# Folding half of an adjacency tile onto the other before it is packed into bits

## The chip, the cores and the metric

The kernel runs on one core of a Trainium2 chip. The metric is the device time of one execution in microseconds. The core has five engines that run their own instruction streams in order and wait for each other on semaphores: TensorE (PE; its weight loads are PEld), VectorE (DVE), ScalarE (ACT), GpSimd (POOL) and SyncE (SP), which here issues the loads.

## What is computed

A graph network of four layers on 4096 nodes with 256 features and one adjacency matrix of 4096 x 4096 int32. Each layer is attention over the neighbours, with a residual sum and a layer norm. Layers 0 and 1 (four heads of 64 features) are what the change touches, with the adjacency matrix's way into the chip:

```
h = x @ W;  e[i, j] = leaky_relu(s_src[i] + s_dst[j])      # per head
e = where(adj == 0, -inf, e)
out = softmax(e, axis=j) @ h
x = layernorm(x + out)
```

Layers 2 and 3 are of the same kind with other score functions and more dense algebra; they read the same adjacency matrix.

## The kernel before

The 4096 rows of the adjacency matrix are 32 tiles t of 128 rows. Each comes in two halves of 128 x 2048 int32 (1 MB) into `adj_in[:, half]`, one buffer for each half, so that SyncE loads half h of tile t only when half h of tile t-1 has been read. **convert(t, half)** (L1724) is one VectorE compare that writes the half as bf16 zeros and ones into `adj_bf[:, t % 2, half]`. **pack_half** (L1320) is 16 TensorE matmuls on 128 x 128 slices of one half against `powers`, identities scaled by powers of two: eight slices add up to a byte, so 32 matmuls (two halves) make a tile's 128 x 512 bytes in one PSUM bank. **store_packed** (L1730 on VectorE for the first tiles, L945 on ScalarE for the others) writes them into `packed`, which stays on the chip for all four layers.

Where this work stands: seven tiles (`PACKED_FIRST`) are converted before attention. Tiles 0 to 4 are packed between the quads of layer 0's projection; `dense(l, q)` is quad q of eight, four tiles of 128 nodes (L1308 with eight score columns appended to the 256 features; L1290 are the transposes for the next quad), whose results ScalarE copies out of PSUM (L876 features, L877 scores). Tiles 5 and 6 are packed after the last quad. The others go three to a **group**: a group is 512 destination nodes of one head, eight units k of 64 matmuls (L1377 and L1380). For every unit VectorE makes two masks (`masks`: edge L1799, pos L1804, neg L1807, in buffers for two units) from the bytes and from `above`, which ScalarE makes (L974). In layer 0's first groups, at = 0 to 7, VectorE has the six converts of three tiles in its program at k = 0 to 5, and TensorE has half a tile's packing after its units k = 1 to 6. Group 8 takes tile 31.

Between projection and first group stands a transition. `masks_ahead` makes the masks of two units; `stats` (L1931 to L1938) takes the largest score and subtracts it, ScalarE raises two exponentials (L909, L910); `first_products` (L1825), `first_rests` (L1834) and `first_lasts` (L1840) make the first attention values in three bf16 parts, with ScalarE's casts (L958) between. Then TensorE starts group 0.

The order on each engine is written out by hand; no scheduler moves anything. The functions that the change touches:

Of the kernel before, what the change touches and what calls it, by code (L numbers as in the profile page):

```python
# [7 lines left out]
ALU = mybir.AluOpType  # L8
# [63 lines left out]
PACKS = 3  # L72

# [100 lines left out]
def gnn_kernel(nc, A, out, last_layer=3):  # L174

    with ExitStack() as ctx:
# [164 lines left out]
        s_hps = sem("h_in_psum")  # L341
        s_h = sem("h_made")
# [228 lines left out]
        def first_tiles(l, u):  # L571

            out = []
            for kind, vtmp in enumerate((vtmp_dve, vtmp_pool)):
                j = slice(u * CHUNK, (u + 1) * CHUNK)
                factor, hd = (emul[:, kind, 0:1, j], 0) if l < 3 else (emul[:, 0, 1:2, j], kind)
                k0 = kind * kind_step(l)
                part = [values[:, 0, j, k0 + i * C:k0 + (i + 1) * C] for i in range(PARTS)]
                out.append((vtmp, factor.rearrange("p a n -> p n a"), h[:, j, hd * D:(hd + 1) * D], part))
            return out  # L580
# [284 lines left out]
        def _(act):  # L865
# [5 lines left out]

            def copy_quad_h(l, q):

                for i in range(QT):
                    act.wait_ge(s_hps, q * QT + (l * T + i + 1))
                    act.activation(h[:, q * QT + i, :], bank[2 + i][:, 0:F], ACT.Copy)  # L876
                    act.activation(scores[:, :, q * QT + i], bank[2 + i][:, F:F + 2 * H], ACT.Copy).then_inc(s_h, 1)  # L877
                    if i % 2 == 1 and q + 1 < QUADS:
                        copy_xT_half(l, q + 1, i // 2)
# [20 lines left out]
            def stats(l):  # L900
# [350 lines left out]
            for l in range(last_layer + 1):  # L1251
# [5 lines left out]
                if l < 3:  # L1257
                    for half in range(2):
                        copy_xT_half(l, 0, half)
                    for q in range(QUADS):  # L1260
                        if l == 1 and q in (0, 2):
                            elu_exp(AHEAD + 3 + q // 2)
                        if l < 2 and q == ROW_AT + 1:
                            copy_row(l)
                        if l < 2 and q > ROW_AT:
                            above_ahead(l, q - ROW_AT - 1)
# [14 lines left out]
        def _(pe):  # L1281
# [11 lines left out]

            def dense(l, q):
# [19 lines left out]
            def pack_half(t, half, b):  # L1314

                pe.wait_ge(s_adjbf, t * 2 + half + 1)
# [46 lines left out]
            def group(l, slot, par, at, packs=(), first=False):  # L1363

                for k in range(BITS):
# [20 lines left out]
                    if 1 <= k <= 2 * len(packs):  # L1386
                        n, half = divmod(k - 1, 2)
                        if half == 0:
# [3 lines left out]
                            else:  # L1392
                                pe.wait_ge(s_banksum, PACKS * (at - 1) + n + 1)
                        pack_half(packs[n], half, GT * (1 - par) + n)
# [292 lines left out]
        def _(dve):  # L1687
# [31 lines left out]
            def convert(t, half):  # L1719

                dve.wait_ge(s_adj[half], (t + 1) * 16)
                if t >= 2:
                    dve.wait_ge(s_packmm, t * 2 + half - 3 + CREDIT)
                dve.tensor_scalar(adj_bf[:, t % 2, half, :], adj_in[:, half, :], 0, None, ALU.is_gt)\  # L1724
                    .then_inc(s_adjbf, 1)
# [83 lines left out]
            def masks_ahead(l):  # L1809
# [4 lines left out]
                for k in range(UNITS_AHEAD):  # L1814
                    for _ in masks(l, TURN[l] * H * UNITS + k, k, packed[:, :, 0:WORDS]):
                        pass

            def first_products(l, u):
# [3 lines left out]
                for vtmp, factor, columns, _ in first_tiles(l, u):  # L1822
# [102 lines left out]
            def stats(l):  # L1925

                n = H if l < 3 else 1
                if l < 3:
                    dve.wait_ge(s_h, T * (l + 1) + 1)
# [73 lines left out]
            def group(l, g, gg, par, banks_before, norm=None, first=False, front=None, fold=None, ahead=None,  # L2003
# [7 lines left out]
                for k in range(BITS):  # L2011
# [14 lines left out]
                    if l == 0 and first and k == 0:  # L2026
                        store_packed(PACKED_WOVEN, 6 + PACKED_WOVEN % 2)
# [14 lines left out]
                    elif k < UNITS_AHEAD:  # L2042
                        if k == 0:
                            first_rests(l, 0)
                            first_lasts(l, 0)
                    else:
# [373 lines left out]
            for l in range(last_layer + 1):  # L2420
                if l == 3:
                    dense2()
                if l == 0:
                    fold_first_weights()
                    for t in range(PACKED_FIRST):
                        for half in range(2):
                            convert(t, half)
# [37 lines left out]
```

## Time and profile before

| what | value |
|---|---|
| time, median of 3 runs | 2997.62 us (2996.97 to 2999.9) |
| the profiled execution: its own time, its span | 2995.74 us, 2993.9 us |
| TensorE matmuls busy | 2923.0 us, 98% of the span |
| VectorE busy | 2133.9 us, 71% |
| ScalarE busy | 1920.6 us, 64% |
| adjacency loads | 64 of 1 MB, median 4.9 us from issue to landing |

The profile is one execution. A share is an average over the span: VectorE's 71% holds stretches of layer 0 where it works nearly all the time, and others where it has little to do. A row of a timeline gives the start, the duration and, in brackets, how long the engine sat idle before it and what it then waited for.

### The profile page before, as it was taken

How to read it: one execution, taken by the hardware profiler on the slowest of the kernel's cores; microseconds unless marked ns; L12 is line 12 of the kernel's file. 1: busy time of each engine (PE TensorE's matmuls, PEld its weight loads, DVE VectorE, ACT ScalarE, POOL GpSimd, SP SyncE). 2: the span in 40 equal slices, each digit the busy share in tenths (PEclk: the TensorE clock that was granted, in tenths of full speed). 3: DMA queues.
4: the chain of work that ended last, by engine and by line, in shares of the span. 5: the costliest groups of instructions: out<-in, count | busy, mean ns of one | idle time of the engine just before them, and what ended most of it. 6: DMA issues, size and time to landing. Idle time of an engine off the chain costs nothing.

```text
span 2993.9 us, 65253 instructions
## 1 busy us (share of the span) xinstructions
PE 2923.0 (98%) x24628; PEld 2556.9 (85%) x24628; DVE 2133.9 (71%) x3887; ACT 1920.6 (64%) x3414; POOL 1179.6 (39%) x1559
## 2 busy tenths in 40 slices
PE   7999999999989999999999999999999999989999
PEld 6899999999979999999998878887788878755555
DVE  5999898888888888888896556566666656562245
ACT  4777999999988999999985545444455444430000
POOL 0672385641226565654121023333323333444222
PEclk9999999999999999999999999999999999999999
DMA  8677100000100000000010000000000000000001
GB/s 292 207 234 246 39 11 15 11 11 14 62 15 13 11 15 11 15 11 15 11 35 12 4 1 4 4 1 4 1 4 4 1 1 1 3 1 1 0 14 42
DMA packets 41912, 104.55 MB, mean 35 GB/s; under 512 B 9856, under 2 KB 23424, under 8 KB 33536
## 3 DMA queue, kind: packets, MB, share of 16 engines
q1 hardware_dynamic: 39616, 101.61, 10.4%
q8 instruction: 111, 1.82, 0.2%
q10 hardware_dynamic: 2112, 0.52, 0.1%
q14 instruction: 73, 0.60, 0.1%
HBM read 97.73 MB, written 4.39 MB: 34 GB/s over the span
## 4 chain that ended last, share of the span: by engine, by line
PE 89%; DVE 5%; ACT 2%; issue 2%; DMA 1%; POOL 1%; SPq 0%; DVEq 0%; POOLq 0%; ACTq 0%
PE bank L1377 21%; PE bank L1380 21%; PE bank L1435 16%; PE bank L1473 13%; PE bank L1383 11%; PE bank L1308 2%; PE bank L1462 2%; DMA arena<-in_adj_dram 1%; PE bank L1449 1%; DVE rings L1804 1%; DVE arena L1724 1%; PE bank L1320 1%; ACT above L974 1%; PE bank L1358 1%; DVE rings L1799 1%
## 5 line engine op out<-in xcount | busy, mean ns | idle before, releaser
L1377 PE MATMUL bank<-values,rings 128*128 128x195 bf16 x8192 | 1392.1, 248 | 31.5 <-DVE rings L1807 19.0
L1380 PE MATMUL bank<-values,rings 128*128 128x195 bf16 x8192 | 1392.0, 248 | 0.0
L974 ACT ACTIVATE above<-srow,kpass 128x512 fp8e4<-128x512 f32 x2032 | 1279.9, 709 | 96.2 <-DVE rings L1807 87.1
L1377 PEld LDWEIGHTS bank<-values,rings 128*128 128x128 fp8e4 x8192 | 802.9, 98 | 44.0 <-issue 39.8
L1380 PEld LDWEIGHTS bank<-values,rings 128*128 128x128 fp8e4 x8192 | 802.9, 98 | 0.4
L1804 DVE TENSOR_TENSOR rings<-rings,above 128x512 uint32<-128x512 uint32 x512 | 387.1, 756 | 171.8 <-PE bank L1380 135.4
L1062 ACT ACTIVATE values<-srow,cmul 128x512 f32<-128x512 f32 x256 | 206.0, 815 | 411.5 <-PE bank L1473 410.5
L1807 DVE TENSOR_TENSOR rings<-rings 128x512 uint32<-128x512 uint32 x512 | 425.7, 831 | 17.3
L1473 PE MATMUL bank<-hv,values 128*128 128x257 f32 x1792 | 420.6, 380 | 0.0
L1473 PEld LDWEIGHTS bank<-hv,values 128*128 128x128 f32 x1792 | 335.0, 190 | 69.9 <-issue 25.2
L1383 PE MATMUL bank<-values,rings 128*128 128x390 bf16 x1920 | 318.7, 329 | 10.1 <-DVE values L1840 10.1
L1383 PEld LDWEIGHTS bank<-values,rings 128*128 128x128 fp8e4 x1920 | 188.3, 98 | 140.5 <-issue 12.4
L633 POOL TENSOR_TENSOR quot<-sums,cmul 128x260 f32<-128x260 f32 x64 | 49.4, 771 | 563.9 <-DVE sums L1960 453.4
L1799 DVE TENSOR_SCALAR rings<-packed 128x512 uint32 (+1 forms) x512 | 260.6, 509 | 2.5 <-ACT packed L945 2.4
L1914 DVE SCALAR_TENSOR_TENSOR values<-values,cmul,rings 128x512 f32<-128x512 f32 x256 | 191.8, 757 | 35.0 <-ACT values L1062 34.4
L766 POOL TENSOR_SCALAR zrow<-zrow 128x1 f32<-128x1 f32 x128 | 45.6, 356 | 429.7 <-DVE zrow L2168 429.7
L2031 DVE TENSOR_SCALAR rings<-packed 128x512 uint32 (+1 forms) x120 | 54.4, 453 | 199.6 <-PE bank L1383 199.5
L1960 DVE TENSOR_REDUCE sums<-bank 128x130 f32<-128x390 f32 x320 | 176.5, 554 | 3.5 <-PE bank L1358 1.7
L1435 PE MATMUL bank<-arena,above 128*128 128x256 f32 (+1 forms) x496 | 165.9, 482 | 0.8 <-ACT above L1117 0.8
L1435 PEld LDWEIGHTS bank<-arena,above 128*128 128x128 f32 x496 | 94.0, 190 | 53.1 <-issue 43.8
L1435 PE MATMUL bank<-quot,arena 128*128 128x256 f32 x512 | 118.3, 379 | 0.0
L562 POOL TENSOR_TENSOR values<-vtmp_pool,values 128x260 f32 (+1 forms) x112 | 105.9, 946 | 21.9 <-POOL values L559 14.5
(223 smaller groups left out, 3483.5 us busy)
## 6 DMA issues: line engine op xcount, KB each, us to landing
arena<-in_adj_dram SPq DMA_DIRECT2D x64, 1024.0 KB, 4.9
srow<-src_dram SPq DMA_DIRECT2D x69, 256.0 KB, 3.1
x<-in_x_dram SPq DMA_DIRECT2D x4, 1024.0 KB, 11.4
out_dram<-x SPq DMA_DIRECT2D x7, 512.0 KB, 2.9
arena<-in_L_gnn_fe_w_dram SPq DMA_DIRECT2D x2, 512.0 KB, 7.2
arena<-in_L_gnn_W_hz_dram SPq DMA_DIRECT2D x1, 1024.0 KB, 7.7
arena<-in_L_gnn_g_w_dram SPq DMA_DIRECT2D x1, 1024.0 KB, 10.9
weights<-in_L_gnn_W_dram SPq DMA_DIRECT2D x3, 256.0 KB, 3.5
```

The source lines that it names most:

```text
L974: last = act.activation(above[:, k % 2, q, :], srow[:, par, :], ACT.Relu, scale=BIG, bias=kpass[:, p % 2, k * Q + q:k * Q + q + 1], satura ...
L1062: act.activation(w2[:, m % DEPTH, :], srow[:, g % 2, :], ACT.Relu, scale=b_col[:, jt:jt + 1], bias=c_neg[:, jt:jt + 1]).then_inc(E.relu, 1)
L1377: pe.matmul(acc[:, 0:KW], pos[:, k % 2, q, :].bitcast(FP8)[:, rows], v[:, 0:KW], start=start, stop=final, skip_group_check=True)
L1380: last = pe.matmul(acc[:, KP:KP + KW], neg[:, k % 2, q, :].bitcast(FP8)[:, rows], v[:, KP:KP + KW], start=False, stop=final, skip_group_ch ...
L1383: last = pe.matmul(acc[:, 0:2 * KW], edge[:, k % 2, q, :].bitcast(FP8)[:, rows], v[:, 0:2 * KW], start=start, stop=final)
L1435: last = pe.matmul(dst, lhsT[k], rhs[k], start=(k == 0), stop=(k == len(lhsT) - 1))
L1473: last = pe.matmul(bank[it][:, 0:VW], w2[:, m % DEPTH, it * P:(it + 1) * P], hv[:, k * Q + q, :], start=(k == 0 and q == 0), stop=False)
L1799: dve.tensor_scalar(edge[:, r], words, shift[0], ONE, shift[1], ALU.bitwise_and).then_inc(s_dve, 1)
L1804: dve.tensor_tensor(pos[:, r], edge[:, r], above[:, r].bitcast(U32), ALU.bitwise_and).then_inc(s_dve, 1)
L1807: dve.tensor_tensor(neg[:, r], edge[:, r], pos[:, r], ALU.bitwise_xor).then_inc(s_sides, 1)
L1914: dve.scalar_tensor_tensor(out=w2[:, m % DEPTH, :], in0=w2[:, m % DEPTH, :], scalar=c_pos[:, jt:jt + 1], in1=edge[:, unit % 2, q, :].bitca ...
L1960: return dve.tensor_reduce(sums[:, slot, it, :, :], parts, AX.X, ALU.add)
```

## The change

Thirteen tiles (0 to 6, and 22, 23, 25, 26, 28, 29) are **folded**. Half 0 is converted as before but scaled by 2^-4. Half 1 is no longer converted by itself: one VectorE instruction (`scalar_tensor_tensor`, called the fold here) compares it and adds the result onto the bf16 tile of half 0, so that each element holds two bits. TensorE then packs 16 slices of that one tile instead of 32, and waits for both halves. In the groups it does so after unit k = 2n+2 for the n-th tile of the group, and nothing after k = 2n+1.

In layers 0 and 1 the last quad's scores are computed by matmuls of their own, 8 columns wide, into bank 6: those of the quad's first two tiles ahead of its features, those of the other two behind the first tile's features. ScalarE copies all four tiles' scores with one instruction, and `stats` waits for that copy instead of for the last features. Bank 6 holds packed tile 4 just before, so in layer 0 these matmuls wait for its store. Tile 6's converts move from ahead of the masks into the transition, `masks_ahead` makes one unit's masks, the second unit's come behind `first_lasts`, and the products start behind the first of the two exponentials. The two stores of the transition stand at its end.

```
+FOLDED_LATE = (22, 23, 25, 26, 28, 29)
+DOWN_HALF = 2.0 ** -(BITS // 2)
+def folded(t):
+    return t < PACKED_FIRST or t in FOLDED_LATE
...
+            def copy_last_scores(l):
+                act.wait_ge(s_scoreps, l + 1)
+                act.activation(scores[:, :, T - QT:T], bank[6][:, 0:QT * 2 * H].rearrange("p (t c) -> p c t", c=2 * H),
+                               ACT.Copy).then_inc(s_lastscores, 1)
...
-                    act.activation(e[:, 1], e[:, 0], ACT.Exp, scale=SLOPES[l])
+                    act.activation(e[:, 1], e[:, 0], ACT.Exp, scale=SLOPES[l]).then_inc(s_expone, 1)
...
+            def scores_first(l, q, tiles):
+                if l == 0:
+                    pe.wait_ge(s_packed, (PACKED_WOVEN - 1) // 2 * 2 + 1 + CREDIT)
+                for i in tiles:
+                    pe.wait_ge(s_xt, q * 2 + (l * 2 * QUADS + i // 2 + 1))
+                    for k in range(2):
+                        last = pe.matmul(bank[6][:, i * 2 * H:(i + 1) * 2 * H], xT[q % 2][:, i, k, :],
+                                         weights[:, k, F:F + 2 * H], start=(i == 0 and k == 0),
+                                         stop=(i == QT - 1 and k == 1), skip_group_check=True)
...
+                last_quad = q == QUADS - 1 and l < 2
+                if last_quad:
+                    scores_first(l, q, (0, 1))
+                    width = F
                 for i in range(QT):
+                    if last_quad and i == 1:
+                        scores_first(l, q, (2, 3))
...
-                pe.wait_ge(s_adjbf, t * 2 + half + 1)
+                pe.wait_ge(s_adjbf, t * 2 + (2 if folded(t) else half + 1))
+                if folded(t):
+                    for k in range(half * (BITS // 4), (half + 1) * (BITS // 4)):
...
+                if folded(t) and half == 0:
+                    dve.tensor_scalar(adj_bf[:, t % 2, 0, :], adj_in[:, 0, :], 0, DOWN_HALF, ALU.is_gt, ALU.mult)\
+                        .then_inc(s_adjbf, 1)
+                elif folded(t):
+                    dve.wait_ge(s_adjbf, t * 2 + 1)
+                    dve.scalar_tensor_tensor(out=adj_bf[:, t % 2, 0, :], in0=adj_in[:, 1, :], scalar=0,
+                                             in1=adj_bf[:, t % 2, 0, :], op0=ALU.is_gt, op1=ALU.add)\
+                        .then_inc(s_adjbf, 1)
...
                     shifted.then_inc(s_shift, 1)
-                    dve.wait_ge(s_exps, l + 1)
+                    if l == 0:
+                        convert(PACKED_FIRST - 1, 0)
+                    dve.wait_ge(s_expone, l + 1)
...
                     if l == 0 and first and k == 0:
-                        store_packed(PACKED_WOVEN, 6 + PACKED_WOVEN % 2)
+                        convert(PACKED_FIRST - 1, 1)
...
                             first_lasts(l, 0)
+                            for _ in masks(l, unit + 1, 1, words):
+                                pass
+                            if l == 0:
+                                store_packed(PACKED_WOVEN, 6 + PACKED_WOVEN % 2)
```

On VectorE, the transition of layer 0 in the kernel before, from the largest score to tile 7's converts (`arena<-arena`; `packed<-bank` are the stores, `values` and `vtmp_pool` the two kinds of first values):

```order
L1938 TENSOR_TENSOR emul<-scores,smax 128x128
L2023 MEMSET credits 128x1
L1824 COPY values<-emul 128x8
L1825 TENSOR_TENSOR values<-hv,emul 128x8x64
L1824 COPY vtmp_pool<-emul 128x8
L1825 TENSOR_TENSOR vtmp_pool<-hv,emul 128x8x64
L1730 CAST packed<-bank 128x4x128
L1834 TENSOR_TENSOR values<-values 128x520
L1834 TENSOR_TENSOR vtmp_pool<-vtmp_pool,values 128x520
L1840 TENSOR_TENSOR values<-values 128x8x65
L1840 TENSOR_TENSOR values<-vtmp_pool,values 128x8x65
L1730 CAST packed<-bank 128x4x128
```

The same place in the changed kernel:

```order
L2003 TENSOR_TENSOR emul<-scores,smax 128x128
L1777 TENSOR_SCALAR arena<-arena 128x2048
L2090 MEMSET credits 128x1
L1888 COPY vtmp_pool<-emul 128x8
L1889 TENSOR_TENSOR vtmp_pool<-hv,emul 128x8x64
L1888 COPY values<-emul 128x8
L1889 TENSOR_TENSOR values<-hv,emul 128x8x64
L1781 SCALAR_TENSOR_TENSOR arena<-arena 128x2048
L1898 TENSOR_TENSOR vtmp_pool<-vtmp_pool,values 128x520
L1898 TENSOR_TENSOR values<-values 128x520
L1904 TENSOR_TENSOR values<-vtmp_pool,values 128x8x65
L1904 TENSOR_TENSOR values<-values 128x8x65
```

Tile 6's compare and fold now stand inside the transition, and the two stores (and the second unit's three mask instructions) come behind these rows.

On TensorE, the last two quads of layer 0's projection in the changed kernel, behind tile 4's packing; the 128x8 rows are the scores by themselves, and the x32 at the end the packing of tiles 5 and 6:

```order
L1360 MATMUL bank<-powers,arena 128x128 x16
L1347 MATMUL bank<-weights,values 128x264 x4
L1310 MATMUL bank<-ident,x 128x128 x4
L1347 MATMUL bank<-weights,values 128x264 x4
L1310 MATMUL bank<-ident,x 128x128 x4
L1321 MATMUL bank<-weights,values 128x8 x4
L1347 MATMUL bank<-weights,values 128x256 x2
L1321 MATMUL bank<-weights,values 128x8 x4
L1347 MATMUL bank<-weights,values 128x256 x6
L1396 MATMUL bank<-ident,scores 128x128
L1360 MATMUL bank<-powers,arena 128x128 x32
```

Before, the same place read x32 for tile 4, eight matmuls of 264 columns for the last quad, and x64 for tiles 5 and 6.

On VectorE, inside group 5 of layer 0, from tile 22's fold to tile 23's; `rings` are the masks, `sums` a reduction of the group before:

```order
L1781 SCALAR_TENSOR_TENSOR arena<-arena 128x2048
L1860 TENSOR_SCALAR rings<-packed 128x512
L1865 TENSOR_TENSOR rings<-rings,above 128x512
L1868 TENSOR_TENSOR rings<-rings 128x512
L2027 TENSOR_REDUCE sums<-bank 128x130
L1777 TENSOR_SCALAR arena<-arena 128x2048
L1860 TENSOR_SCALAR rings<-packed 128x512
L1865 TENSOR_TENSOR rings<-rings,above 128x512
L1868 TENSOR_TENSOR rings<-rings 128x512
L2027 TENSOR_REDUCE sums<-bank 128x130
L1781 SCALAR_TENSOR_TENSOR arena<-arena 128x2048
```

Each of the two folds stands where a compare stood, ahead of the masks of k = 2 and of k = 4; nothing else moved on VectorE there.

## Rows read from the trace of the kernel before

**Rows 1.** The page's first part, and its chain that ended last, by engine.

```profile
PE 2923.0 (98%) x24628; PEld 2556.9 (85%) x24628; DVE 2133.9 (71%) x3887; ACT 1920.6 (64%) x3414; POOL 1179.6 (39%) x1559
...
PE 89%; DVE 5%; ACT 2%; issue 2%; DMA 1%; POOL 1%; SPq 0%; DVEq 0%; POOLq 0%; ACTq 0%
```

**Rows 2.** Stretches of layer 0: length, busy PE, PEld, DVE, ACT, POOL, clock, DMA.

```profile
100.00:150.00 50.00, 45.26 (x577) 43.87 (x574) 48.79 (x59) 37.85 (x63) 42.49 (x53) 1.00 0.57 186
...
233.40:260.30 26.90, 26.90 (x356) 26.90 (x353) 23.90 (x35) 21.48 (x35) 5.45 (x5) 1.00 0.75 245
```

**Rows 3.** What VectorE waits for, 20 to 63 and 74 to 206 us.

```profile
DVE arena L1724 <- DMA arena<-in_adj_dram: 26.7, 14, 3.9
...
DVE rings L1799 <- ACT packed L945: 2.4, 1, 2.4
...
DVE rings L1804 <- PE bank L1380: 0.2, 1, 0.2
```

**Rows 4.** The chain of waits, 20 to 64 us: start, us, what.

```profile
50.52 4.75 DMA arena<-in_adj_dram
...
55.30 1.24 DVE arena L1724
...
56.55 5.47 DMA arena<-in_adj_dram
```

**Rows 5.** VectorE's timeline over the transition of layer 0.

```profile
62.05 1.23 DVE L1724 TENSOR_SCALAR arena<-arena 128x2048 bf16<-128x2048 int32 x1 [2.65 <-DMA arena<-in_adj_dram]
...
66.77 0.28 DVE L1931 TENSOR_REDUCE smax<-scores 128x4 f32<-128x128 f32 x1
...
68.49 0.17 DVE L1824 COPY values<-emul 128x8 f32<-128x8 f32 x1 [0.58 <-issue]
...
70.44 0.69 DVE L1834 TENSOR_TENSOR values<-values 128x520 f32<-128x520 f32 x1
...
73.06 0.68 DVE L1730 CAST packed<-bank 128x512 uint8<-128x512 f32 x1
73.66 2.60 DVE L1724 TENSOR_SCALAR arena<-arena 128x2048 bf16<-128x2048 int32 x2
```

**Rows 6.** TensorE's timeline over the last quad and the start of group 0.

```profile
58.74 0.49 PE L1290 MATMUL bank<-ident,x 128*128 128x128 f32 x3
59.07 3.73 PE L1308 MATMUL bank<-weights,values 128*128 128x264 f32 x16
63.34 0.33 PE L1348 MATMUL bank<-ident,scores 128*128 128x128 f32 x1 [0.55 <-ACT scores L877]
...
73.25 0.32 PE L1377 MATMUL bank<-values,rings 128*128 128x195 bf16 x1 [6.00 <-issue]
```

**Rows 7.** VectorE's groups of instructions, whole span: busy us, mean ns | idle before.

```profile
L1724 DVE TENSOR_SCALAR arena<-arena 128x2048 bf16<-128x2048 int32 x64 | 80.4, 1257 | 26.7 <-DMA arena<-in_adj_dram 26.7
...
L2185 DVE SCALAR_TENSOR_TENSOR above<-vtmp_pool,above 128x512 f32<-128x512 f32 x62 | 41.2, 683 | 26.1 <-ACT vtmp_pool L1100 25.0
...
L1737 DVE SCALAR_TENSOR_TENSOR values<-values,hv 128x1024 f32<-128x1024 f32 x8 | 9.7, 1218 | 0.2 <-ACT values L893 0.2
```

**Rows 8.** VectorE's timeline in group 5: masks of k = 0, 1 and 5.

```profile
224.57 0.69 DVE L1804 TENSOR_TENSOR rings<-rings,above 128x512 uint32<-128x512 uint32 x1 [1.38 <-PE bank L1380]
...
228.49 0.69 DVE L1804 TENSOR_TENSOR rings<-rings,above 128x512 uint32<-128x512 uint32 x1 [1.03 <-ACT above L974]
...
243.53 1.11 DVE L1807 TENSOR_TENSOR rings<-rings 128x512 uint32<-128x512 uint32 x1
```

**Rows 9.** The chain of waits in group 5: half a tile packed behind unit 4.

```profile
244.16 0.89 PE bank L1320 x16
```

**Rows 10.** A short idle time of TensorE (its timeline), and the window behind it.

```profile
91.94 0.32 PE L1377 MATMUL bank<-values,rings 128*128 128x195 bf16 x1 [2.38 <-DVE rings L1807]
...
92.00:94.00 2.00, 2.00 (x13) 1.86 (x14) 1.97 (x3) 2.00 (x4) 0.00 (x0) 0.50 0.13 16
```

**Rows 11.** TensorE's timeline in layer 1's transition: the first matmul of group 0.

```profile
874.18 0.32 PE L1377 MATMUL bank<-values,rings 128*128 128x195 bf16 x1 [5.73 <-DVE values L1840]
```

More of the change, by code:

```diff
@@ L1264, in _ @@
                             copy_row(l)
+                        if l < 2 and q == QUADS - 1:
+                            copy_last_scores(l)
                         if l < 2 and q > ROW_AT:
@@ L1292, in x_across @@
                 last.then_inc(s_xtps, 1)
+            def scores_first(l, q, tiles):
[7 more added lines that the diff above has]
+                                         stop=(i == QT - 1 and k == 1), skip_group_check=True)
+                if tiles[-1] == QT - 1:
+                    last.then_inc(s_scoreps, 1)
             def dense(l, q):
@@ L1314, in pack_half @@
             def pack_half(t, half, b):
-                pe.wait_ge(s_adjbf, t * 2 + half + 1)
+                pe.wait_ge(s_adjbf, t * 2 + (2 if folded(t) else half + 1))
+                if folded(t):
+                    for k in range(half * (BITS // 4), (half + 1) * (BITS // 4)):
+                        for q in range(Q):
+                            j = k * Q + q
+                            last = pe.matmul(bank[b][:, q * P:(q + 1) * P], adj_bf[:, t % 2, 0, j * P:(j + 1) * P],
+                                             powers[:, BITS // 2 + k, :], start=(k == 0 and q == 0),
+                                             stop=(k == BITS // 2 - 1 and q == Q - 1), skip_group_check=True)
+                    last.then_inc(s_packmm, 1)
+                    return
                 for k in range(half * (BITS // 2), (half + 1) * (BITS // 2)):
@@ L1387, in group @@
                         n, half = divmod(k - 1, 2)
-                        if half == 0:
+                        if folded(packs[n]) and half == 0:
+                            continue
+                        if half == 0 or folded(packs[n]):
                             if at == 0:
@@ L1813, in masks_ahead @@
                     dve.wait_ge(s_packed, GT + CREDIT)
-                for k in range(UNITS_AHEAD):
-                    for _ in masks(l, TURN[l] * H * UNITS + k, k, packed[:, :, 0:WORDS]):
-                        pass
+                for _ in masks(l, TURN[l] * H * UNITS, 0, packed[:, :, 0:WORDS]):
+                    pass
             def first_products(l, u):
@@ L1821, in first_products @@
                     dve.wait_ge(s_vrest, first_values_before(l) + 2 * u)
-                for vtmp, factor, columns, _ in first_tiles(l, u):
+                if l < 2 and u == FIRST_CHUNKS - 1:
+                    dve.wait_ge(s_h, T * (l + 1) + 1)
+                for i, (vtmp, factor, columns, _) in enumerate(first_tiles(l, u)):
+                    if l < 2 and u == 0 and i == 1:
+                        dve.wait_ge(s_exps, l + 1)
                     big = vtmp[:, 0]
@@ L2426, in _ @@
                         for half in range(2):
-                            convert(t, half)
+                            if t < PACKED_FIRST - 1:
+                                convert(t, half)
                         if 1 <= t <= PACKED_WOVEN:
```

23 lines of the change are left out of this document (16 added, 7 removed).

## The prediction

> **What bounds the kernel now.** The page comes first: TensorE is busy for 98% of the span and holds 89% of the chain that ended last [rows 1]. By that, 7 microseconds of matmuls taken off would be 7 off the time. The share is an average, so I look next at stretches. Between 100 and 150 us TensorE works 45.26 of 50 us and VectorE 48.79; from 233.4 to 260.3, in group 5 of layer 0, it is TensorE with all of 26.90, and VectorE has 23.90 [rows 2]. So layer 0 has two parts. In the early one VectorE is the bound: from 74 to 206 us it waits in five places for 4.5 us in all, the first and last of which are 2.4 for a store by ScalarE and 0.2 for TensorE [rows 3]. In the late one TensorE is, with about 3 us of VectorE's left over in a group. Ahead of both stands the loading, 20 to 63 us, where VectorE waits 26.7 us, 14 times, for adjacency halves [rows 3]. The chain of waits there alternates between two things, a load of half 1 (six between 4.75 and 5.88, the shortest shown) and the compare of that half, 1.24 [rows 4]: the next load into the one buffer starts only when VectorE has read the last. What VectorE does with half 0 is not on this chain, and what it does with half 1 is.
>
> **What a fold costs.** The compare it takes the place of has 1.22 to 1.26 us for 2048 elements. The trace has no fold with an int32 and a bf16 source; the nearest rows are scalar_tensor_tensor with two f32 sources, 683 ns for 512 elements and 1218 for 1024 [rows 7], so 1.045 ns an element, and 1.218 + 1024 x 0.001045 = 2.29 us for 2048. From below, the fold could cost what the compare does. I take 2.29, the price of the same instruction: 1.06 more each. Seven folds stand early and six late, 13 x 1.06 = 13.8 us of VectorE's work, against 13 x 16 = 208 fewer matmuls of TensorE's, at 0.89 for 16 [rows 9] 11.6 us. The scaled compare of half 0 has one more operation on the same elements; I cost it as the compare.
>
> Both f32 rows come to about one element in a nanosecond. The Trainium skill (Vector Engine (DVE) Microarchitecture Reference, section 7, points that are easy to get wrong) says that this instruction with two sources in SBUF that are not bf16 has its throughput halved. It speaks against the change; by it, were the int32 source enough, a fold would take some 4.4 us. The L1737 row, with two f32 sources, shows 1218 ns for 1024 elements, no halving against the 512 row.
>
> **Early part, layer 0.** Fold by fold: tile 5's half 1 was ready at 55.30 [rows 4]. Five folds (tiles 0 to 4) stand ahead of its load on that chain. Were each wholly added, it comes 5.3 later; as the two halves' loads then overlap less, each load may shrink towards the shortest, by up to 0.5, which leaves 2.8. I take 0.9 a tile, 4.5: ready at 59.8 (58.1 to 60.6). Its fold ends at 62.0, and the store of tile 4 behind it takes 0.60 (from 73.06 to 73.66) [rows 5]: 62.6.
>
> TensorE comes sooner to the last quad. Tile 4's fold ends one cycle of the chain earlier (4.75 + 1.24 before, 0.9 more now), at 55.1; 16 packing matmuls, 0.9, and quad 6, 16 records at 0.223 and eight transposes at 0.11 [rows 6], 4.45, bring it to 60.4. There it has to wait for the store of tile 4, about 2.2 us, since the scores go into the same bank. What packing saves ahead of that (five times 0.9) is so spent in waiting for folds.
>
> A matmul of eight columns isn't in the trace: between nothing and the 0.22 of a record of 264 columns. I take 0.11, that of a transpose record [rows 6], 0.87 for the eight records of two tiles. From 62.6: scores 0.87, first tile 0.89, scores 0.87, so 65.3; ScalarE's copy 0.4, 65.7 (the wait for the copy was 0.55 before) [rows 6]. One unit's masks took 1.79 (two between the convert that starts at 62.05 and 66.77), so they are done. From largest score to shifted scores it was some 1.13 (from 66.77 to the start of the wait of 0.58 that ends at 68.49) [rows 5]: 66.9. Tile 6's compare stands next, 1.14, to 68.05. The exponential should have run beside it, but on ScalarE it stands behind the four feature copies, and the quad's matmuls end at 65.3 + 2.7 = 68.05. So the products start at 68.7, against 68.49: the early scores buy nothing. Products 1.35, fold of tile 6 2.2, to 72.25; rests and lasts with their gap 2.6 (from 70.44 to 73.06) [rows 5], to 74.8, where TensorE starts, against 73.25. Then the second masks, 1.8, and two stores, 1.2: tile 7's compare at 77.8 instead of 73.66. **+4.1**, from +2.4 (loads shrink all they can) to +6. It stays, since VectorE has no idle time behind it to give it back [rows 3].
>
> **Late groups.** Groups 5, 6 and 7 each have two folds. VectorE has 23.90 + 2.12 = 26.0 us of work a group, TensorE 26.9 - 1.8 = 25.1. VectorE's idle time sits at the start: 1.38 for TensorE to give back a mask buffer, 1.03 for ScalarE [rows 8]; from k = 2 on it waits for nothing. In the middle it is just in time: the masks of k = 5 end at 243.53 + 1.11 = 244.64, TensorE ends its packing behind unit 4 at 245.05 [rows 8, 9], 0.4 later. Two folds put these masks at 246.76, so unit 5 starts 1.7 later; units 6 and 7, and the next group's first wait on them, follow. The wait for ScalarE may shrink, its work being 21.48 of 26.90 [rows 2]: I take +1.4 a group, **+4.2** for three. From above: 5.7, nothing taken up and a little more. From below: VectorE without any wait, 26.0 against 26.9, is -0.9 a group, -2.6.
>
> **Layer 1** has no packing. TensorE's first group waited 5.73 us for the products [rows 11]. The scores come earlier, the exponentials still stand behind the feature copies, and 16 score records add up to 1.75; the second unit's masks, made in idle time before, come behind `first_lasts`. **+0.5**, from -0.7 to +1.5.
>
> **Sum.** 4.1 + 4.2 + 0.5 = +8.8 on the profiled execution's 2995.74 us: 3004.5. The median of the runs is 1.9 higher: **3006.4 us**. A measurement of this kernel can tell about 0.2%, 6 us, from no change.
>
> **Rivals.** *The late waits absorb the folds* (0.25): VectorE's 2.4 us of waiting in a group take the 2.1 that two folds add, as VectorE falls behind and finds buffers free. What decides is whether these waits are for something that moves along; the 1.38 is for TensorE's unit 6, which I say moves. Then a group is 26.5, -0.4, and the sum 4.1 - 1.2 + 0.5 = +3.4: 3001, not slower by what can be told.
> *The clock falls ahead of the last quad* (0.08): an idle time of 2.38 us was followed by a granted clock of 0.50 [rows 10], and I forecast one of 2.2. The projection's first matmuls at the lower of the two levels cost some 1.6 more: 3008.
> *A fold costs no more than the compare* (0.09): the early chain stays, about +0.4; the late groups are TensorE's, -1.8 each; layer 1 as above: -4.5, 2993.
> *TensorE is the bound throughout* (0.06), as its 98% says: 11.6 us of packing come off, 2986. Against it stands VectorE's 48.79 of 50.
> *The fold runs at half the pace of the f32 rows* (0.02): 2048 x 1.045 ns, 2.1 us, more than I took for each of the five early folds in the chain of loads, for tile 6's and for the six late ones, 25 us on top: 3032. The f32 rows speak against it. The Trainium skill's rule named above would be its reason.
>
> **How the numbers follow.** My forecast has 0.50, and spans 3001 to 3012 by its bounds, most of it above 3003.6, the mark of 0.2%. Slower: 0.42 of it, the clock's 0.08 and the halved fold's 0.02, 0.52. Same: the rest of the forecast 0.08, the late waits 0.25, half the cheap fold, 0.37. Faster: the other half and TensorE as the bound, 0.11. The range leaves out the cheap fold, TensorE's bound and the halved fold: 2996 to 3011.
>
> **What would show it.** The fold's row: 2.3 us. The chain of waits before 63 us with folds of 2.3 in it and loads of about 5.1; TensorE idle for some 2 us ahead of the 8-column matmuls, waiting for VectorE's store; the products at about 68.7, tile 7's compare at about 77.8. In groups 5 to 7 TensorE idle in front of units 2, 4 and 5, waiting for masks, and a period of 28.3 instead of 26.9. I am wrong if the fold's row is near 1.2, if loads shrink by as much as folds grow, or if VectorE's waits at k = 0 and k = 1 vanish and TensorE's groups come every 26.5 or less.

## The result, and the profile after

| what | before | after |
|---|---|---|
| median of the runs | 2997.63 us (2996.97 to 2999.9, 6 runs) | 3013.19 us (3010.03 to 3015.15, 6 runs) |
| ratio | | 1.005, 95% interval 1.004 to 1.006 |
| the profiled execution, its span | 2995.74 us, 2993.9 us | 3012.15 us, 3010.3 us |

Slower, by 15.6 us (0.5%) where 8.8 were forecast, and outside the range. The page after, its first part and its chain by engine, hardly differs from [rows 1]: VectorE has 14.7 us more to do. TensorE has 176 matmuls fewer (208 of packing less 32 of scores) and is busy no shorter, since more of its work ran at the lower clock, as will be seen.

```profile
PE 2924.2 (97%) x24452; PEld 2556.1 (85%) x24452; DVE 2148.6 (71%) x3887; ACT 1921.4 (64%) x3408; POOL 1180.8 (39%) x1559
...
PE 87%; DVE 7%; issue 2%; ACT 2%; DMA 1%; POOL 1%; SPq 0%; DVEq 0%; POOLq 0%; ACTq 0%
```

Where the time went is read off VectorE's timeline in both kernels: the last mask instruction of each unit (L1807, now L1868) is the n-th of its kind in either, so the difference of their starts is the delay at that place. It grows at three places. After the transition of layer 0 it is 7.97 us, 9.25 at the end of group 0 and through group 4; in each of the groups 5, 6 and 7 it grows by 2.02; at layer 1's transition by 0.83. With 0.3 behind that, it is the 16.4 by which the spans differ.

The fold's row among VectorE's groups of instructions, to be held against the compare in [rows 7]:

```profile
L1781 DVE SCALAR_TENSOR_TENSOR arena<-arena 128x2048 bf16<-128x2048 int32 x13 | 29.7, 2287 | 15.3 <-DMA arena<-in_adj_dram 15.3
```

2.287 us, where 2.29 was forecast. The chain of waits over the loading, where [rows 4] were:

```profile
53.20 2.31 DVE arena L1781
55.51 0.02 issue
55.52 4.78 DMA arena<-in_adj_dram
...
62.53 0.69 DVE packed L1791
63.23 0.04 issue
63.27 0.83 PE bank L1321 x6
```

Tile 5's half 1 came at 60.32 (59.8 forecast), and the chain goes from its fold to the store of tile 4 and from there to the 8-column matmuls on TensorE, as the prediction had it. What TensorE then did, in its timeline, and one window of that stretch with the granted clock (the third figure from the end):

```profile
63.27 1.07 PE L1321 MATMUL bank<-weights,values 128*128 128x8 f32 x8 [2.08 <-DVE packed L1791]
64.20 2.06 PE L1347 MATMUL bank<-weights,values 128*128 128x256 f32 x4
66.05 1.72 PE L1321 MATMUL bank<-weights,values 128*128 128x8 f32 x8
67.61 4.50 PE L1347 MATMUL bank<-weights,values 128*128 128x256 f32 x12
...
79.14 0.32 PE L1425 MATMUL bank<-values,rings 128*128 128x195 bf16 x1 [1.53 <-issue]
```

```profile
66.00:68.00 2.00, 2.00 (x10) 1.95 (x9) 0.00 (x0) 0.20 (x2) 0.00 (x0) 0.50 0.36 152
```

TensorE waited 2.08 us, and the clock, at 1.00 for about another microsecond, then stood at 0.50, the lower of its two levels, for most of the quad. The last quad took from 63.27 to 72.1, 8.8 us instead of the 5.45 forecast (62.6 to 68.05). VectorE's timeline, the rows that answer to [rows 5], shows that this was waited for:

```profile
68.10 0.29 DVE L1996 TENSOR_REDUCE smax<-scores 128x4 f32<-128x128 f32 x1 [3.10 <-ACT scores L885]
...
72.78 0.17 DVE L1888 COPY vtmp_pool<-emul 128x8 f32<-128x8 f32 x1 [2.40 <-issue]
...
74.13 2.28 DVE L1781 SCALAR_TENSOR_TENSOR arena<-arena 128x2048 bf16<-128x2048 int32 x1
...
82.02 2.44 DVE L1785 TENSOR_SCALAR arena<-arena 128x2048 bf16<-128x2048 int32 x2
```

It idles 3.10 us for the scores and 2.40 in front of the products, and tile 7's compare stands at 82.02: 8.4 later than in [rows 5], and 4.2 later than forecast. In group 6, VectorE's two waits (as in [rows 8]) are still there. The second is for `above`, which ScalarE makes behind its store of the group's third packed tile, and that store has itself waited for TensorE's packing (the ACT row). TensorE now has three waits of its own, ahead of units 2, 4 and 5; the window is that group's whole period:

```profile
262.74 0.69 DVE L1865 TENSOR_TENSOR rings<-rings,above 128x512 uint32<-128x512 uint32 x1 [1.38 <-PE bank L1428]
...
266.66 0.69 DVE L1865 TENSOR_TENSOR rings<-rings,above 128x512 uint32<-128x512 uint32 x1 [1.03 <-ACT above L992]
```

```profile
263.53 0.60 ACT L963 ACTIVATE packed<-bank 128x512 uint8<-128x512 f32 x1 [1.64 <-PE bank L1368]
```

```profile
272.69 0.24 PE L1425 MATMUL bank<-values,rings 128*128 128x195 bf16 x1 [1.11 <-DVE rings L1868]
280.54 0.24 PE L1425 MATMUL bank<-values,rings 128*128 128x195 bf16 x1 [1.41 <-DVE rings L1868]
...
285.08 0.24 PE L1425 MATMUL bank<-values,rings 128*128 128x195 bf16 x1 [0.79 <-DVE rings L1868]
```

```profile
262.74:291.66 28.92, 25.60 (x324) 25.05 (x322) 26.03 (x34) 21.82 (x35) 5.46 (x5) 1.00 0.67 228
```

Before, the period was 26.90, all of it TensorE's [rows 2]; now it is 28.92, with TensorE busy for 25.60; the three waits are the difference.

### The profile page after: what moved, and what is told of

Its sections match the earlier page's. It is cut to its first block, busy times and chain, and to the rows that moved or that the text cites. A ratio compares the mean times of both kernels' runs of the same rounds, so it can differ in the third digit from the quotient of the medians.

```text
span 3010.3 us, 64901 instructions
## 1 busy us (share of the span) xinstructions
PE 2924.2 (97%) x24452; PEld 2556.1 (85%) x24452; DVE 2148.6 (71%) x3887; ACT 1921.4 (64%) x3408; POOL 1180.8 (39%) x1559
## 4 chain that ended last, share of the span: by engine, by line
PE 87%; DVE 7%; issue 2%; ACT 2%; DMA 1%; POOL 1%; SPq 0%; DVEq 0%; POOLq 0%; ACTq 0%
PE bank L1425 20%; PE bank L1428 20%; PE bank L1487 16%; PE bank L1525 13%; PE bank L1431 11%; PE bank L1347 2%; PE bank L1514 2%; DVE rings L1865 2%; PE bank L1501 1%; DMA arena<-in_adj_dram 1%; ACT above L992 1%; DVE rings L1860 1%; DVE arena L1785 1%; DVE arena L1781 1%; DVE rings L1868 1%
## 5 line engine op out<-in xcount | busy, mean ns | idle before, releaser
L1868 DVE TENSOR_TENSOR rings<-rings 128x512 uint32<-128x512 uint32 x512 | 426.2, 832 | 17.3
L1431 PEld LDWEIGHTS bank<-values,rings 128*128 128x128 fp8e4 x1920 | 188.2, 98 | 140.8 <-issue 12.5
```

The costliest lines, as they stand in the source:

```text
L1431: last = pe.matmul(acc[:, 0:2 * KW], edge[:, k % 2, q, :].bitcast(FP8)[:, rows], v[:, 0:2 * KW], start=start, stop=final)
L1868: dve.tensor_tensor(neg[:, r], edge[:, r], pos[:, r], ALU.bitwise_xor).then_inc(s_sides, 1)
```

## The experiments

**Theories.** A: of the early delay, what goes beyond the forecast is the low clock in the last quad. Against it, B: only the wait for the store counts, and C: the new order of the transition is itself the cost. V: the late groups run in a loop through VectorE whose period was 26.8 us all along (28.92 less 2 x 1.06), its two waits included, just under TensorE's 26.9. Against it, S: TensorE is their bound and VectorE has time left.

For all runs together, from VectorE's timelines: the start of the last mask of unit 2 (behind the transition), that of unit 40 (the first of group 5), and the period of groups 5, 6 and 7.

| kernel | unit 2 | unit 40 | periods | median against before on the same chip |
|---|---|---|---|---|
| before | 81.45 | 225.29 | 26.91 26.91 26.90 | |
| changed | 89.42 | 234.54 | 28.92 28.93 28.92 | +15.6 |
| again | 86.57 | 231.87 | 28.93 28.93 28.92 | +14.6 |
| filled | 84.74 | 230.05 | 28.92 28.93 28.92 | +12.5 |
| other_bank | 85.39 | 230.32 | 28.93 28.93 28.93 | +9.6 |
| plain_compare | 83.60 | 227.72 | 26.79 26.81 26.79 | +2.1 |
| scores_only | 81.00 | 226.86 | 26.91 26.91 26.90 | +1.5 |
| early_only_old_transition | 87.88 | 232.50 | 26.90 26.91 27.45 | +8.7 |
| late_only | 80.22 | 224.71 | 28.92 28.93 28.93 | +5.8 |
| first_of_three | 82.04 | 227.28 | 27.87 27.87 27.87 | +3.8 |
| third_of_three | 81.31 | 225.17 | 27.62 27.68 28.05 | +3.7 |
| in_the_wait_none | 81.65 | 226.96 | 26.91 26.90 26.91 | +0.9 |
| in_the_wait_one | 80.64 | 224.40 | 26.02 26.01 26.01 | -2.0 |
| in_the_wait_two | 83.83 | 229.15 | 26.91 26.91 26.91 | +1.0 |

The periods repeat to 0.02 us within a kernel, but for third_of_three and the last one of early_only_old_transition (27.45, for which no run shows a cause). The early columns don't repeat like that: seven kernels (before, late_only and the five of the last rows) have the same program up to group 4, and unit 2 stands there between 80.22 and 83.83, unit 40 between 224.40 and 229.15, means 81.6 and 226.1. The spread is there before the transition: the last adjacency half that VectorE waits for came between 60.87 and 64.47 in these seven. A difference of 2 us in these columns, in single executions, is none.

**filled.** TensorE is kept at work while it waits, and nothing else is changed:

```
+FILL = 40
...
+                if last_quad and l == 0:
+                    pe.wait_ge(s_packed, PACKED_WOVEN - 1 + CREDIT)
+                    for n in range(FILL):
+                        pe.matmul(bank[7][:, 0:P], powers[:, 0, :], powers[:, 1, :], start=True, stop=True,
+                                  skip_group_check=True)
                 if last_quad:
                     scores_first(l, q, (0, 1))
```

Expected:

> The changed kernel, with 40 matmuls of 128 x 128 (bf16, into bank 7, which nobody reads then) ahead of the last quad's score matmuls in layer 0, so that TensorE works through most of the 2.08 us in which it now waits for tile 4's store; everything else waits as in the changed kernel. Theory A, the clock: the changed kernel's last quad ran from 63.27 to 72.1 us, 8.8 us, because the granted clock was 0.50 there; at full clock it takes 5.5. Then the products start some 3.3 earlier than 72.78, tile 7's compare stands near 78.8 instead of 82.1, and the delay of group 4's masks against the kernel before falls from 9.25 to 6 or, if the low clock of group 0 goes too, to 4.7; span 3005.5 to 3007. Theory B, the wait alone: what counts is when the store comes, and the stretched matmuls lie beside other work; then the span stays at 3010.

TensorE's timeline:

```profile
59.33 2.40 PE L1339 MATMUL bank<-powers 128*128 128x128 bf16 x40
61.93 1.06 PE L1322 MATMUL bank<-weights,values 128*128 128x8 f32 x8 [0.20 <-DVE packed L1797]
...
64.60 2.84 PE L1353 MATMUL bank<-weights,values 128*128 128x256 f32 x12
67.91 0.33 PE L1402 MATMUL bank<-ident,scores 128*128 128x128 f32 x1 [0.47 <-ACT hv L893]
```

The quad takes 61.93 to 67.4, 5.5 us, at full clock; unit 2 is 4.7 earlier than in the changed kernel. 1.3 of that is not the clock's: in this execution tile 5's half 1 came at 58.98 instead of 60.32. What is left, 3.3, is the difference in the quad's length. B falls, and the medians agree: 3.1 less than in the changed kernel. The span, 3007.8, is above the 3005.5 to 3007 expected.

**other_bank.** The scores no longer wait for tile 4's store:

```
-                    pe.wait_ge(s_packed, (PACKED_WOVEN - 1) // 2 * 2 + 1 + CREDIT)
+                    pe.wait_ge(s_packed, PACKED_WOVEN - 1 + CREDIT)
...
-                        last = pe.matmul(bank[6][:, i * 2 * H:(i + 1) * 2 * H], xT[q % 2][:, i, k, :],
+                        last = pe.matmul(bank[7 - l][:, i * 2 * H:(i + 1) * 2 * H], xT[q % 2][:, i, k, :],
```

Expected:

> The changed kernel, with the last quad's scores of layer 0 in bank 7 instead of bank 6, so that they wait for tile 3's store, long done, instead of tile 4's. Theory A, the clock: TensorE reaches the last quad at 61.2 and goes straight on at full clock, ends it at 66.7, products at about 67.4, tile 7's compare at 76.6 against 73.66 before: the early delay falls from 9.25 to about 3 to 4, span 3004 to 3005. Theory B, the wait alone: 2.1 less, span 3008.2. Rival C, the new order of the transition (tile 6's compare and fold and the second unit's masks inside it) is the main cost: the early delay stays above 6.

TensorE goes into the quad without a wait and at full clock:

```profile
61.32 0.96 PE L1321 MATMUL bank<-weights,values 128*128 128x8 f32 x8
...
63.89 2.84 PE L1347 MATMUL bank<-weights,values 128*128 128x256 f32 x12
```

Unit 2 is 4.0 earlier than in the changed kernel, unit 40 4.2; span 3007.5 where 3004 to 3005 was expected. In this execution tile 5's half 1 came only at 61.96, 1.6 later than in the changed kernel's; from there VectorE waits 0.34 us in all up to tile 7's compare at 77.99 (76.6 expected). So the delay left, 3.8 against the mean of the seven, holds the folds, the new order and that late load, and no more wait for TensorE.

**plain_compare.** Half 1 of the thirteen tiles is converted as before, and the packing stays at 16 slices, so this kernel leaves half 1's edges out of the bits:

```
-                elif folded(t):
-                    dve.wait_ge(s_adjbf, t * 2 + 1)
-                    dve.scalar_tensor_tensor(out=adj_bf[:, t % 2, 0, :], in0=adj_in[:, 1, :], scalar=0,
-                                             in1=adj_bf[:, t % 2, 0, :], op0=ALU.is_gt, op1=ALU.add)\
-                        .then_inc(s_adjbf, 1)
```

Expected:

> The changed kernel, but the second half of the thirteen tiles is converted by the plain compare of before, into its own tile; TensorE still packs 16 slices, of half 0 alone, so half 1's edges of these tiles are left out of the bits. It takes the 1.06 us of each fold away and keeps what TensorE saves. Theory V for the late groups (VectorE's own loop, with its waits at k = 0 and k = 1 that move along, has a period of 28.92 - 2.12 = 26.8 us, and TensorE's 26.9 was only just longer): the groups 5 to 7 come every 26.8, -0.1 each, although TensorE has 1.8 less to do. Rival S (TensorE is their bound and VectorE has time left): 25.1 each, -5.4 for three. Early: without the folds the chain of loads is that of before, tile 4's store is done at 57.2, the last quad ends at 62.7, tile 7's compare at 71.5 against 73.66, -2. Span by V 2992.5, by S 2987.

Period 26.8, as V had it, and not the 25.1 of S. One group's window:

```profile
254.51:281.32 26.81, 25.61 (x323) 25.06 (x321) 23.93 (x35) 21.73 (x35) 5.45 (x5) 1.00 0.74 246
```

TensorE has 1.2 us idle here and VectorE 2.9, and still the groups come no faster: neither's work alone is the period. The early part was expected 2 us ahead of before and was 2 behind (span 2998.0 for 2992.5), by the same mishap as in the changed kernel: TensorE waited for the store, and the quad ran at the low clock.

```profile
58.53 1.27 PE L1321 MATMUL bank<-weights,values 128*128 128x8 f32 x8 [2.39 <-DVE packed L1786]
...
63.06 4.31 PE L1347 MATMUL bank<-weights,values 128*128 128x256 f32 x12
```

**scores_only.** No folds:

```
 def folded(t):
-    return t < PACKED_FIRST or t in FOLDED_LATE
+    return False
```

Expected:

> The changed kernel without any fold: all tiles are converted and packed as before, and only the last quad's scores and the new order of the transition are left. Theories A and V: the chain of loads is that of before, TensorE reaches the last quad at 59.1, does not wait for tile 4's store (57.1), products at 65.2, tile 7's compare at 73.3, -0.4 against before; layer 1 +0.8; span 2994 to 2995. Rival C, the transition's new order is the main early cost by itself: tile 7's compare at 77 or later, span 2998 or more.

Products at 65.42, tile 7's compare at 73.60 against 73.66 before: C falls as a main cost. The span, 2997.1, is above the 2994 to 2995 expected, and short of C's 2998. Unit 4's masks were 0.80 behind, where unit 2's were 0.45 ahead; the changed kernel has the same step of 1.25 (7.97 to 9.22), and the kernel with the old transition has not. It is a stretch at the low clock again. TensorE's timeline at unit 2 and a window behind it, in the changed kernel, and the same place in plain_compare:

```profile
90.20 0.24 PE L1425 MATMUL bank<-values,rings 128*128 128x195 bf16 x1 [1.96 <-DVE rings L1868]
```

```profile
92.00:94.00 2.00, 2.00 (x14) 1.83 (x13) 1.97 (x3) 0.70 (x2) 0.00 (x0) 0.50 0.85 213
```

```profile
84.39 0.24 PE L1425 MATMUL bank<-values,rings 128*128 128x195 bf16 x1 [3.20 <-DVE rings L1863]
```

```profile
86.00:88.00 2.00, 2.00 (x32) 2.00 (x30) 1.97 (x3) 0.88 (x2) 0.00 (x0) 1.00 0.78 180
```

From unit 3's last mask to unit 4's it takes 7.9 to 8.1 us in the five kernels whose clock is at 0.50 there, and 6.8 in the nine where it is at 1.00: the step is the clock's. Of the six kernels with the new order, five have it; plain_compare has not, though its TensorE had waited longer. The kernel before pays the same a little later, behind its wait of 2.38 ahead of unit 4 [rows 10]. By unit 40 scores_only is within the spread of the seven.

**early_only_old_transition.** The kernel before with `convert` and `pack_half` of the change for tiles 0 to 6, and nothing else:

```
+FOLDED = (0, 1, 2, 3, 4, 5, 6)
+def folded(t):
+    return t in FOLDED
```

Expected:

> The kernel before with tiles 0 to 6 folded and nothing else of the change: the last quad has its scores with its features, and tile 6's compare and fold stand ahead of the masks as before. Theory A: the chain of loads is that of the changed kernel up to tile 5 (its half 1 at 60.3), and goes on to tile 6, whose fold ends at 69.8 instead of 63.2; all behind it is 6.6 later, tile 7's compare at 80.3, and the early delay is 6.6, or 7.9 if group 0 again has a stretch at the low clock; so the new transition by itself costs rather than saves, by the wait for the store and the clock, 9.25 against 6.6. Rival (the new transition saves what it was to save): the early delay here is above 9.25. Span 3000.5 to 3002.

The chain goes on to tile 6, in VectorE's timeline:

```profile
60.20 2.29 DVE L1750 SCALAR_TENSOR_TENSOR arena<-arena 128x2048 bf16<-128x2048 int32 x1 [2.37 <-DMA arena<-in_adj_dram]
...
67.46 2.29 DVE L1750 SCALAR_TENSOR_TENSOR arena<-arena 128x2048 bf16<-128x2048 int32 x1 [3.23 <-DMA arena<-in_adj_dram]
69.67 0.42 DVE L1829 TENSOR_SCALAR rings<-packed 128x512 uint32<-128x512 uint32 x1
```

Masks at 69.67 instead of 63.19, +6.48, tile 7's compare at 80.14 (span 3003.3 for 3000.5 to 3002). Seven folds on the chain of loads cost that much with the old transition. At unit 2, against the mean of the seven, it is 6.3 here, 3.8 for the new transition without its wait (other_bank), and 7.8 and 5.0 with it (changed, again). An estimate from the medians says the same: take late_only's 5.8 off, and the new transition is at 3.8 without the wait and at 9.8 and 8.8 with it, layer 1's part included, where the old one is at 8.7. So the new transition is of use, and the wait for the store, with the clock, takes about all of it back.

**late_only, first_of_three, third_of_three.** The same with other tiles: `FOLDED = (22, 23, 25, 26, 28, 29)`, `(22, 25, 28)` and `(24, 27, 30)`. Expected:

> The kernel before with the six late tiles folded (22, 23, 25, 26, 28, 29) and nothing else of the change. Theory V (a loop through VectorE sets the period of groups 5 to 7, and all of 2 x 1.06 a group appears, less the 0.1 by which TensorE was longer): period 28.9 us against 26.9, +2.0 a group, +6.1 in all; TensorE waits for masks ahead of units 2 and 4. My own step (TensorE just late for unit 5, the rest taken up): +1.4 a group, +4.2. Rival (the waits at k = 0 and k = 1 absorb the folds): -0.4 a group, -1.2.

> The kernel before with only the first tile of each of the groups 5 to 7 folded (22, 25, 28): its fold stands ahead of the masks of k = 2, and TensorE packs 16 slices behind unit 2 and none behind unit 1. Theory V: the loop 26.8 + 1.06 = 27.9 a group, +0.96 each, +2.9 in all. Rival (VectorE's 2.4 us of waiting in a group take up one fold, and TensorE's 0.9 comes off): 26.0 to 26.4 a group, -1.5 to -2.7.

> The kernel before with only the third tile of each of the groups 5 to 7 folded (24, 27, 30): its fold stands behind the masks of k = 5, and TensorE packs 16 slices behind unit 6 and none behind unit 5. Theory V says that the loop runs through VectorE up to k = 5 and from there through TensorE's units 5 and 6 and their packing to ScalarE's store and the masks of k = 1; so this fold is off it but for the masks of k = 6, and the 0.9 taken off behind unit 5 is on it: unit 6 waits for masks 1.06 later, some 0.3 later than before. Period 26.9 to 27.2, 0 to +0.8 in all, against +2.9 for the first of three. Rival (a fold costs its 1.06 wherever it stands): +2.9, as the first of three. Rival (TensorE is the bound): -0.9 a group, -2.7.

28.92 and 27.87 are V's numbers (28.9, 27.9). The third was missed: 27.6 to 28.1 where 26.9 to 27.2 was expected. TensorE's timeline at unit 6:

```profile
249.07 0.24 PE L1394 MATMUL bank<-values,rings 128*128 128x195 bf16 x1 [1.45 <-DVE rings L1837]
```

TensorE did come 0.9 earlier to unit 6, and waited 1.45 for its masks. I had taken the masks of k = 6 to have some 0.8 us to spare; in the kernel before they end at 247.85 and unit 6 starts at 248.48, 0.6. So a fold costs 0.7 to 1.1 us in this place too. That fits V if its loop's exit is a unit later than I put it; no run tests this by itself.

**in_the_wait_none, in_the_wait_one, in_the_wait_two.** If VectorE's two waits in a group are part of the loop, work put into them is free. The first tile's two converts move up, in groups 5 to 7:

```
+EARLY_CONVERT = (5, 6, 7)
...
-                        for _ in masks(l, unit, k, words):
+                        made = masks(l, unit, k, words)
+                        next(made)
+                        if front is not None and k < 2 and g in EARLY_CONVERT:
+                            convert(packs_of(g)[k // 2], k % 2)
+                        for _ in made:
                             pass
...
-                        if k < 2 * len(packs_of(g)):
+                        if k < 2 * len(packs_of(g)) and not (k < 2 and g in EARLY_CONVERT):
```

with no fold, with tiles 22, 25, 28 folded, and with the six. Expected:

> The kernel before without any fold; in the groups 5 to 7 the first tile's two converts stand behind the edge mask of k = 0 and of k = 1 instead of behind these units' last masks, so that VectorE makes them in the 1.4 and 1.0 us in which it waits. Theory V: VectorE's loop is shorter by the second of them, 26.8 - 1.14 = 25.7, but TensorE has 26.9 of work: the period stays 26.9, nothing in all. A control for the next two.

> As the run before, with one tile of each of the groups 5 to 7 folded (22, 25, 28), its fold in the wait of k = 1. Theory V: VectorE's loop is 25.7, the fold costs nothing there, and TensorE's 26.9 - 0.9 = 26.0 is the bound: -0.9 a group, -2.7 in all, where the same folds without the move cost +2.9. Rival (a fold costs its 1.06 in VectorE's total work, wherever it stands): 27.9, as without the move.

> As the run before, with two tiles of each of the groups 5 to 7 folded, as in the changed kernel; the second fold stands ahead of the masks of k = 4, inside the loop. Theory V: 25.7 + 1.06 = 26.8 a group by VectorE, 25.1 by TensorE: -0.1 a group, -0.4 in all, against +6.1 without the move. Rival (TensorE's matmuls set the period once the waits are filled): 25.1, -5.4 in all.

26.9, 26.0 and 26.9: V to 0.1 us in all three. One group's window with one fold in the wait, and what is left of the waits in VectorE's timeline:

```profile
250.42:276.43 26.01, 26.01 (x339) 26.01 (x337) 24.94 (x35) 21.38 (x35) 5.45 (x5) 1.00 0.75 254
```

```profile
249.69 0.69 DVE L1835 TENSOR_TENSOR rings<-rings,above 128x512 uint32<-128x512 uint32 x1 [0.36 <-PE bank L1398]
256.06 0.69 DVE L1835 TENSOR_TENSOR rings<-rings,above 128x512 uint32<-128x512 uint32 x1 [0.22 <-ACT above L983]
```

Here the 0.9 us that TensorE saves per fold come off, because the fold stands where VectorE had nothing to do. This version has the lowest time of all: 2995.10 us median against 2997.14, ratio 0.9993 (0.9984 to 1.0002). The 2.7 us are plain in the trace and too small for the runs to tell from none.

**again.** The changed kernel once more. Expected:

> The changed kernel itself once more, for how much of its early delay is the program's and how much one execution's. The kernels whose program is that of before up to group 4 had the masks that open the second group (unit 8) between 105.25 and 110.65 us in their profiled executions; the changed kernel had them at 115.85. Theory A: TensorE again idles some 2 us ahead of the last quad's score matmuls, and the quad again runs at a granted clock of 0.50 and takes 8 to 9 us, since the wait is in the program; unit 8's masks at 113 to 118. If it were an accident of that execution, the quad takes 5.5 and unit 8's masks stand near 111.9, as with the scores in another bank.

The ratio was 1.0049 (1.0026 to 1.0072), but the last quad ran at full clock:

```profile
55.98 1.05 PE L1360 MATMUL bank<-powers,arena 128*128 128x128 bf16 x16 [3.00 <-DVE arena L1781]
56.88 3.62 PE L1347 MATMUL bank<-weights,values 128*128 128x264 f32 x8
...
63.76 1.06 PE L1321 MATMUL bank<-weights,values 128*128 128x8 f32 x8 [0.54 <-DVE packed L1791]
...
66.43 2.84 PE L1347 MATMUL bank<-weights,values 128*128 128x256 f32 x12
```

Here TensorE had waited 3.00 us for tile 4's fold, ran the quad before the last at the low clock (3.62 us for 8 records that took 1.95 otherwise), and so came late enough to wait only 0.54. Where TensorE idles ahead of the last quad depends on when the loads of that execution land. The early delay (unit 40 against the mean of the seven) was 5.7 here and 8.4 in the other execution; I had expected the low clock on the last quad in both. The whole spans differ by only 0.6 us: near 1620 us, behind layer 1, this execution falls back by another 1.7, filled does so too, and the execution shown above does not. A single execution's time is therefore no measure of the clock's price; the quad's own length is.

## Why the prediction was wrong

The direction was right, and so were most steps of the working. Two failed: that the last quad runs at full clock, and that a third of what the folds add to a late group is taken up, 0.4 us by the time to spare at unit 5 and the rest by a shorter wait of VectorE for ScalarE.

- *What a fold costs*: right. 2.287 us measured, 2.29 forecast. The Trainium skill's rule cited there (Vector Engine (DVE) Microarchitecture Reference, section 7, points that are easy to get wrong) asks for two sources that are not bf16, and the fold has one; the estimate of some 4.4 holds only were one enough. The comparison of 512 with 1024 elements in the prediction could not show a halving, since both rows have two f32 sources. What speaks against one is tensor_tensor with two f32 sources, 0.69 us for 520 elements [rows 5], the pace of the 683 ns for 512 [rows 7]; the fold, with an int32 and a bf16 source, keeps that pace.
- *The chain of loads*: right in kind. Tile 5's half 1 at 60.32, 60.20, 58.98, 60.81 and 61.96 in five executions with these folds (changed, early_only_old_transition, filled, again, other_bank), where 58.1 to 60.6 was forecast: three inside, two late.
- *The wait for tile 4's store*: right, 2.08 us for 2.2 forecast, and it goes away when the bank does. That the size was met is in part luck: it was 0.54 in again.
- *The last quad at full clock*: wrong in the execution shown. I had its clock as a rival at 0.08 and 1.6 us, on the ground of a row in which an idle time of 2.38 us was followed by 0.50. It happened, and cost 3.3 by filled, since the quad ran at the lower level for most of its length, and ScalarE's copies, the products and all behind them waited for its end. At unit 2, against the mean of the seven, the early term was 7.8 and 5.0 in two executions for 4.1 forecast. 3.3 of the first is the last quad's clock; what is left, 4.5 and 5.0, is over the forecast by less than executions differ among themselves. By unit 40 another 1.3 and 1.5 were lost against the kernel before (0.6 and 0.7 against the mean), beginning with the low clock behind unit 2's wait (1.25), a term that the prediction put at nothing.
- *Late groups, "the wait for ScalarE may shrink"*: wrong. I took 1.4 of a possible 2.1 a group, and it was 2.02, 6.1 in all for 4.2. VectorE's waits of 1.38 and 1.03 stayed to the hundredth, since they are for TensorE's unit 6 and for ScalarE behind its store of packed bytes, and both follow from VectorE's masks of the same group. My step took the lateness at unit 5 alone, 1.7, by holding VectorE's masks against TensorE's times of before, where TensorE still had the half packs that the folds take away; without them, TensorE waits for units 2 and 4 too, and the 0.4 to spare is gone. The rival in which these waits absorb the folds (0.25) is refuted by late_only; in_the_wait_one shows that they can take up work that is put into them.
- *Layer 1*: +0.83 for +0.5, but the seven kernels and early_only_old_transition, whose layer 1 is that of before, differ by -0.1 to +1.3 at this place, so the runs do not tell it from none.
- *The cheap fold, and TensorE as the bound*: refuted, the first by the fold's row and the second by plain_compare, where the -1.8 a group that the packing saves came to -0.1.

Open: what decides whether the clock falls behind a wait. On the last quad there are two executions of the changed kernel, one with the low clock and one without, and in group 0 it stayed up behind a wait of 3.20 us and fell behind shorter ones.

## What to carry to other kernels

When two engines hand work back and forth, idle time of the one inside the loop is no reserve: it moves along with whatever is added. Look at what each wait is for, follow that back, and if it leads to the same engine's earlier work, count added work in full, or put it into the wait itself. And a wait of some 2 us on TensorE is to be priced with the matmuls behind it at the lower clock too, as a case with a real chance, when somebody waits for them.

## What the runs showed of the hardware that was not expected

TensorE's granted clock fell to 0.50 behind idle times of 2.08 (changed), 2.39 (plain_compare) and 3.00 us (again) in the projection, and of 1.96 in group 0 of the changed kernel. It stayed at 1.00 behind one of 1.68 in filled, and also behind 3.20 in group 0 of plain_compare, so the length of the idle time alone does not tell. In filled, 40 matmuls in the idle time went with a clock of 1.00 throughout. A matmul of 8 columns with its two f32 sources took 0.11 us a record at full clock (eight records from 63.76 to 64.67), half of one of 264 columns, which was the guess. Executions of the same program up to there differ by up to 3.6 us behind the transition, as much as the landing of the last adjacency half that VectorE waits for ahead of it (60.87 to 64.47).
